# One exponential per head, a unit's matmuls moved behind the first score tile, and a feature stage in three passes

## Time and profile before

| | |
|---|---|
| median of 3 runs | 3821.25 us (3820.65 to 3821.79) |
| the profiled execution, its own time | 3822.36 us |
| its span in the profile | 3820.6 us |
| busy shares of the span | PE 95%, DVE 75%, ACT 59%, PEld 49%, POOL 12% |

### The profile page before, as it was taken

One profiled execution on the slowest core, in us unless ns is written; L12 is line 12 of the kernel. 1 busy time (PEld: TensorE's weight loads), 2 busy tenths in 40 slices (PEclk: granted clock), 3 DMA queues, 4 the chain that ended last, 5 costly groups with the idle time before them and its releaser, 6 DMA issues.

```text
span 3820.6 us, 65042 instructions
## 1 busy us (share of the span) xinstructions
PE 3613.8 (95%) x24697; PEld 1864.0 (49%) x24697; DVE 2863.1 (75%) x5691; ACT 2268.2 (59%) x2644; POOL 451.4 (12%) x486
## 2 busy tenths in 40 slices
PE   5999999999999977999999997799999999999999
PEld 3445444444444433555555555244545444454545
DVE  6878878778777776777777776487777878778775
ACT  4666666666666514666666652566666666666664
POOL 2000000000000002332323221000000000000000
PEclk9999999999999988999999997799999999999999
DMA  1000000000000000000000000000000000000000
GB/s 48 8 9 10 10 9 10 9 10 10 7 10 7 15 5 4 15 16 13 16 16 11 13 15 2 22 5 11 8 9 10 10 9 11 9 8 11 7 10 15
DMA packets 43631, 43.05 MB, mean 11 GB/s; under 512 B 16210, under 2 KB 30298, under 8 KB 43066
## 3 DMA queue, kind: packets, MB, share of 16 engines
q1 hardware_dynamic: 43322, 38.88, 3.4%
HBM read 36.38 MB, written 1.69 MB: 10 GB/s over the span
## 4 chain that ended last, share of the span: by engine, by line
PE 86%; DVE 6%; ACT 3%; issue 2%; SPq 1%; DMA 1%; POOL 1%; DVEq 0%; POOLq 0%
PE ps L592 82%; ACT work L1084 1%; DVE x L1557 1%; PE ps L929 1%; DVE over L1379 1%; PE ps L940 1%; SPq L499 1%; DMA auxQ<-mrow 1%; DVE wexp L1379 1%; PE ps L969 0%; DVE V L1287 0%; ACT Kh L1044 0%; DVE stats L1275 0%; ACT wexp L1099 0%; ACT over L1099 0%
## 5 line engine op out<-in xcount | busy, mean ns | idle before, releaser
L1356 DVE TENSOR_TENSOR acc<-acc,work 128x1024 f32<-128x1024 f32 (+2 forms) x1152 | 1386.4, 1203 | 62.0 <-ACT work L1084 18.0
L1084 ACT ACTIVATE work<-ps 128x1024 f32<-128x1024 f32 (+1 forms) x1344 | 1276.1, 996 | 201.2 <-PE ps L592 191.6
L592 PE MATMUL ps<-work,V 128*64 128x512 f32 (+3 forms) x5376 | 1233.1, 579 | 0.0
L1379 DVE CUSTOM_DVE_ANT_0 over<-ps,over,mpart 128x512 f32<-128x512 f32 (+3 forms) x642 | 423.3, 697 | 506.8 <-PE ps L592 499.9
L592 PEld LDWEIGHTS ps<-work,V 128*64 128x64 f32 x5376 | 448.9, 137 | 539.7 <-issue 444.5
L592 PE MATMUL ps<-Qh,Kh 64*128 64x512 f32 (+3 forms) x2688 | 659.0, 485 | 36.9 <-ACT work L1084 10.2
L1069 ACT ACTIVATE over<-ps 128x1024 f32<-128x1024 f32 (+1 forms) x321 | 315.9, 984 | 571.5 <-PE ps L592 571.5
L592 PE MATMUL ps<-Qh,Kl 64*128 64x512 f32 (+3 forms) x2688 | 526.8, 386 | 0.0
L592 PE MATMUL ps<-Ql,Kh 64*128 64x512 f32 (+3 forms) x2688 | 523.8, 384 | 0.0
L592 PE MATMUL ps<-auxQ,auxK 64*128 64x512 bf16 (+3 forms) x2688 | 519.7, 380 | 0.0
L1379 DVE CUSTOM_DVE_ANT_0 wexp<-ps,wexp 128x512 f32<-128x512 f32 (+1 forms) x632 | 377.0, 635 | 41.9 <-POOL wexp L1207 16.2
(11 more groups left out here) (190 smaller groups left out, 2749.6 us busy)
## 6 DMA issues: line engine op xcount, KB each, us to landing
rden<-inverse_sums SPq DMA_DIRECT2D x186, 128.0 KB, 2.9
auxQ<-mrow SPq DMA_DIRECT2D x384, 1.0 KB
wqk<-in_wqk SPq DMA_DIRECT2D x24, 128.0 KB, 2.5
dcomp<-rden SPq DMA_DIRECT2D x186, 2.0 KB
wv<-in_wv SPq DMA_DIRECT2D x24, 64.0 KB, 2.2
inverse_sums<-rcomp SPq DMA_DIRECT2D x93, 4.0 KB, 1.3
work<-in_mlp_w SPq DMA_DIRECT2D x1, 1024.0 KB
work<-in_c_aux SPq DMA_DIRECT2D x1, 1024.0 KB, 4.8
```

Source lines behind the costliest of these rows:

```text
L592: return pe.matmul(o, w, m, start=start, stop=stop, skip_group_check=True)
L1084: act.activation(work[:, 2 * e:2 * e + 2, q0:CH], ps[:, b:b + 2, q0:CH], ACT.Exp, scale=L.scale).then_inc(s["p_ready"], 1)
L1356: dve.tensor_tensor(o, o, work[:, slots[two]:slots[two] + 2, q0:CH], ALU.add).then_inc(s["acc_ready"], 1)
L1379: dve.tensor_tensor_reduce(clipped[:, h2, col:col + w], ps[:, b0 + h2, col:col + w], clipped[:, h2, col:col + w], 1.0, start, ALU.add, ALU ...
```

## The change

It has four parts.

1. On TensorE the excess of slot 0 goes behind tile 0, and on ScalarE its Relu goes behind the exponentials of tile 0 (ahead of those of tile 1).
2. A tile's exponentials are two instructions of 512 columns, one for each head. The eight matmuls of a tile are issued as head 0, head 0, head 1, head 0, head 1, head 0, head 1, head 1, and each head has its own increment of `st_ready`. The counts of `st_ready` and `p_ready` are doubled. In tiles 2 and 3 head 0 waits for its own exponential alone, head 1 for its own.
3. The feature stage does all Gelus, then all Sigmoids, then all copies, with buffers of their own for each chunk and six PSUM banks in turn for the first matmuls. Its `softmax(faw)` moves to the experts of the first layer.
4. SP's DMAs of the feature stage move into the opening of the last attention, behind the loads of the first weights.

```diff
 scores():
-    for m, (kk, qq) in enumerate(((Kh, Qh), (Kh, Ql), (Kl, Qh))):
-        for h2 in range(2):
-            mm(ps[:, 2 * two + h2, q0:CH], kk[p][head(h2), keys], qq[p][head(h2), queries], m == 0, False)
-    for h2 in range(2):
-        ins = mm(ps[:, 2 * two + h2, q0:CH], auxK[head(h2), keys], auxQ[p][head(h2), queries], False, True)
-    ins.then_inc(s["st_ready"], 1)
+    if free is not None:
+        pe.wait_ge(s["p_ready"], 2 * free - 1)
+    part(0, 0)
+    part(1, 0)
+    if free is not None:
+        pe.wait_ge(s["p_ready"], 2 * free)
+    part(0, 1)
+    part(2, 0)
+    part(1, 1)
+    part(3, 0).then_inc(s["st_ready"], 1)
+    part(2, 1)
+    part(3, 1).then_inc(s["st_ready"], 1)
 row_block():
-    if 0 in units:
-        m, u = units[0]
-        at_least(pe, s["top_ready"], L.NTOP * m + L.tops_to[u])
-        excess(m, m % 2, u, MAXB)
...
     scores(n, p, 2 * g, 0)
-    at_least(pe, s["p_ready"], tiles)
+    if 0 in units:
+        m, u = units[0]
+        at_least(pe, s["top_ready"], L.NTOP * m + L.tops_to[u])
+        excess(m, m % 2, u, MAXB)
+    at_least(pe, s["p_ready"], 2 * (tiles))
...
     if 0 in units:
         m, u = units[0]
         pe.wait_ge(s["relu_ready"], L.NR * m + L.relus_to[u] + 1)
         base(m, m % 2, u)
-    pe.wait_ge(s["p_ready"], tiles + 1)
-    scores(n, p, 2 * g + 1, 0)
-    pe.wait_ge(s["p_ready"], tiles + 2)
-    scores(n, p, 2 * g + 1, 1)
+    scores(n, p, 2 * g + 1, 0, tiles + 1)
+    scores(n, p, 2 * g + 1, 1, tiles + 2)
 ScalarE, cycle():
-    clip(0)
     if L.main(x):
         for j in range(4):
+            if j == 1:
+                clip(0)
...
-            act.activation(work[:, 2 * e:2 * e + 2, q0:CH], ps[:, b:b + 2, q0:CH], ACT.Exp,
-                           scale=L.scale).then_inc(s["p_ready"], 1)
+            act.activation(work[:, 2 * e, q0:CH], ps[:, b, q0:CH], ACT.Exp, scale=L.scale)\
+                .then_inc(s["p_ready"], 1)
+            act.wait_ge(s["st_ready"], 2 * tile + 2)
+            act.activation(work[:, 2 * e + 1, q0:CH], ps[:, b + 1, q0:CH], ACT.Exp, scale=L.scale)\
+                .then_inc(s["p_ready"], 1)
 TensorE, features():
-    pe.wait_ge(fw_ready, 1)
-    pe.transpose(ps[0:NF, 7, 0:HEADS], faw[:, 0:NF], ident[0:HEADS, 0:HEADS]).then_inc(fwT_psum, 1)
     pe.wait_ge(yt_ready, 7 * NC)
     for c in range(NC):
         for m in range(3):
...
+            at_least(pe, ft_ready, 3 * c + m - 5)
+            pe.matmul(ps[0:M, (3 * c + m) % 6, :], wext[:, m * P:m * P + M], yv[:, c * CH:(c + 1) * CH],
                       start=True, stop=True).then_inc(ft_psum, 1)
+    pe.wait_ge(fw_ready, 1)
+    pe.transpose(ps[0:NF, 7, 0:HEADS], faw[:, 0:NF], ident[0:HEADS, 0:HEADS]).then_inc(fwT_psum, 1)
+    pe.wait_ge(fw_ready, 2)
+    for c in range(NC):
+        pe.wait_ge(ft_ready, 3 * c + 3)
...
+    for c in range(NC):
+        pe.wait_ge(fs_ready, c + 1)
+        pe.matmul(ps[0:HEADS, 4 + c, :], fawT[:], fs[c], start=True, stop=True).then_inc(br_psum, 1)
 ScalarE, ahead of the last attention:
     for c in range(NC):
         for m in range(3):
...
+            act.activation(fh[c][m][0:M, :], ps[0:M, (3 * c + m) % 6, :], ACT.Gelu, bias=bext[0:M, m:m + 1])\
+                .then_inc(ft_ready, 1)
+    for c in range(NC):
+        act.wait_ge(fo_psum, c + 1)
+        act.activation(fs[c], ps[0:NF, (6 + c) % 8, :], ACT.Sigmoid, bias=b2ext[:]).then_inc(fs_ready, 1)
+    for c in range(NC):
         act.wait_ge(br_psum, c + 1)
...
+        act.activation(brow[c], ps[0:HEADS, 4 + c, :], ACT.Copy, scale=1.0 / LAYERS[2].scale).then_inc(br_ready, 1)
 SyncE, attention(), opening():
     load_pair(0, 0)
     load_out(0, 0)
     if L.featured:
+        bias_rows()
         load_bias(0, 0)
```

More of the change, by code:

```diff
@@ L344, in program @@
         small = over[:].rearrange("p m (n t e) -> p (m n) t e", t=NT, e=E_EXP)
-        brow, fs = acc[0:HEADS, 0, 0, :], acc[0:NF, 0, 1, :]
-        bparts = acc[0:HEADS, 1, 0, :].bitcast(BF16).rearrange("h (m q) -> h m q", m=2)
+        fh = [[work[:, slot if slot < 8 else slot + NC, :] for slot in range(3 * c, 3 * c + 3)] for c in range(NC)]
+        fs = [acc[0:NF, c // 2, c % 2, :] for c in range(NC)]
+        brow = [(over if c < 2 else oT)[0:HEADS, c % 2, :] for c in range(NC)]
+        bparts = [acc[0:HEADS, c // 2, c % 2, :].bitcast(BF16).rearrange("h (m q) -> h m q", m=2) for c in range(NC)]
         bT = [wm[0:2 * TPC, p, :].rearrange("r (c q) -> r c q", q=P) for p in range(2)]
@@ L557, in _ @@
             sp.wait_ge(A[1]["x_added"], NC * PAIRS)
[L558 to L566, removed]
             attention(LAYERS[2])
@@ L641, in job, with scores @@
                         ins.then_inc(s["op_ready"], 1)
-                def scores(n, p, k, two):
+                def scores(n, p, k, two, free=None):
                     c, tiles = L.steps[k]
@@ L966, in features @@
                         M = P if m < 2 else FH
-                        if c >= 1:
-                            pe.wait_ge(ft_ready, 4 * (c - 1) + m + 1)
-                        pe.matmul(ps[0:M, m, :], wext[:, m * P:m * P + M], yv[:, c * CH:(c + 1) * CH],
+                        at_least(pe, ft_ready, 3 * c + m - 5)
+                        pe.matmul(ps[0:M, (3 * c + m) % 6, :], wext[:, m * P:m * P + M], yv[:, c * CH:(c + 1) * CH],
                                   start=True, stop=True).then_inc(ft_psum, 1)
-                    pe.wait_ge(ft_ready, 4 * c + 3)
+                pe.wait_ge(fw_ready, 1)
[3 more added lines that the diff above has]
+                    pe.wait_ge(ft_ready, 3 * c + 3)
                     for m in range(3):
                         M = P if m < 2 else FH
[L974 to L980, removed]
+                        mm = pe.matmul(ps[0:NF, (6 + c) % 8, :], w2b[0:M, m, :], fh[c][m][0:M, :], start=(m == 0), stop=(m == 2))
+                    mm.then_inc(fo_psum, 1)
+                for c in range(NC):
+                    pe.wait_ge(fs_ready, c + 1)
+                    pe.matmul(ps[0:HEADS, 4 + c, :], fawT[:], fs[c], start=True, stop=True).then_inc(br_psum, 1)
             pe.wait_ge(ident_in, 16)
@@ L1077, in cycle @@
                             e = tile % RING
[L1078 removed]
+                            act.wait_ge(s["st_ready"], 2 * tile + 1)
                             if tile >= RING:
@@ L1116, in _ @@
             act.wait_ge(dl_ready, 1)
+            act.activation(faw[:, 0:NF], faw[:, 0:NF], ACT.Exp).then_inc(ex_ready, 1)
+            act.wait_ge(dl_ready, 2)
             act.activation(small[:, 2, :, :], small[:, 1, :, :], ACT.Exp).then_inc(ex_ready, 1)
@@ L1140, in _ @@
             whole_norm(6)
-            act.wait_ge(dl_ready, 2)
-            act.activation(faw[:, 0:NF], faw[:, 0:NF], ACT.Exp).then_inc(ex_ready, 1)
             for c in range(NC):
@@ L1145, in _ @@
                     M = P if m < 2 else FH
-                    act.wait_ge(ft_psum, 4 * c + m + 1)
-                    if c >= 1:
-                        act.wait_ge(ft_psum, 4 * c)
-                    act.activation(work[0:M, m, :], ps[0:M, m, :], ACT.Gelu, bias=bext[0:M, m:m + 1]).then_inc(ft_ready, 1)
-                act.wait_ge(ft_psum, 4 * c + 4)
-                act.activation(fs, ps[0:NF, 3, :], ACT.Sigmoid, bias=b2ext[:]).then_inc(ft_ready, 1)
+                    act.wait_ge(ft_psum, 3 * c + m + 1)
+                    act.activation(fh[c][m][0:M, :], ps[0:M, (3 * c + m) % 6, :], ACT.Gelu, bias=bext[0:M, m:m + 1])\
[3 more added lines that the diff above has]
+                act.activation(fs[c], ps[0:NF, (6 + c) % 8, :], ACT.Sigmoid, bias=b2ext[:]).then_inc(fs_ready, 1)
+            for c in range(NC):
                 act.wait_ge(br_psum, c + 1)
-                if c >= 1:
-                    act.wait_ge(br_out, 32 * c)
-                    act.wait_ge(bp_ready, 2 * c)
-                act.activation(brow, ps[0:HEADS, 4, :], ACT.Copy, scale=1.0 / LAYERS[2].scale).then_inc(br_ready, 1)
+                act.activation(brow[c], ps[0:HEADS, 4 + c, :], ACT.Copy, scale=1.0 / LAYERS[2].scale).then_inc(br_ready, 1)
             attention(LAYERS[2])
@@ L1546, in experts @@
                 dve.tensor_tensor(sm[5], sm[0], sm[3], ALU.mult).then_inc(mask_ready, 1)
+                link(dve.tensor_reduce(faw[:, 6:7], faw[:, 0:NF], AX.X, ALU.add))
+                link(dve.reciprocal(faw[:, 7:8], faw[:, 6:7]))
+                dve.tensor_scalar(faw[:, 0:NF], faw[:, 0:NF], faw[:, 7:8], None, ALU.mult).then_inc(fw_ready, 1)
                 dve.wait_ge(mask_ready, 2)
```

48 lines of the change are left out of this document (28 added, 20 removed).

## The result

The changed kernel takes **4109.5 us** (median of 4 runs, 4108.2 to 4113.9) where the one before takes 3821.0 in the same runs (4 runs, 3820.0 to 3821.8). The ratio is 1.0757, with a 95% interval of 1.0739 to 1.0776: 288.5 us slower. The forecast was 4123, in a range of 4030 to 4260.

A forecast was written before the change was run, and what follows sets the result against it. TensorE (PE) was taken as the bound, with 86% of the span. The profiled 3822.4 us +256 (full layers) +67 (causal layer) -21 (features) gave 4124, set to 4123 us for the runs' median; range 4030 to 4260.

The forecast's parts named there:

- The row part: Block from first to last excess: base of slot 0 waits for its late Relu, 5.35 us becomes 6.39, 1.04 us longer.
- The column part: Part of a block behind the row part: claimed to wait for nothing that the change moves, so no cost.
- The full layers' sum: Two full attention layers: 246 blocks with a wide Relu, each 1.04 us longer, +256 us (222 to 310).
- The causal layer: Causal attention layer: wide and narrow Relus +47 and +18, covered `tops` waits -12, GpSimd's cut +14; +67 us (20 to 100).
- The features: Feature stage: engines no longer take turns, first projection 21.4 us earlier, table loads counted as nothing; -21 us (-27 to -14).
- A: Rival, row part: base never waits for the Relu and finer waits close the holes; 3690 us, chance 0.08.
- both holes: PE's waits for ScalarE in each block, ahead of tile 2 and the excess of slot 1; 147 us over about 320 blocks.
- the price of a hole: PE time lost where a weight load waits for ScalarE: 0.23 us each, though the wait reads 0.39.
- B: Rival, score tiles: the shifted heads' matmuls don't pair, so a tile costs five slots; +154 us, 4277 us, chance 0.06.
- C: Rival, score tiles: weight loads of the same half are serial, 511 us, of which half or more shows; 4420 us, chance 0.04.

The follow-up runs named there:

- e9: The changed kernel with the excess of slot 0 ahead of tile 0 again, its Relu still behind tile 0's exponentials: 4193.8 us (one run).
- e7: The changed kernel with the Relu of slot 0 ahead of tile 0's exponentials again, its excess still behind tile 0: 4032.5 us.
- e1: The changed kernel with part 1 undone, excess and Relu of slot 0 first again: 3777.4 us, ratio 0.9882 to the kernel before.
- e6: The changed kernel with the Relu of slot 0 done twice in a row, the second one counted: 4688.7 us (one run).
- e12: The changed kernel with the base of slot 0 behind tile 2 instead of ahead of it: 4069.9 us (one run).
- e10: The kernel before with only parts 3 and 4 added and its own semaphore counts kept: 3802.1 us, ratio 0.9955.
- e5: e1 with the two heads' matmuls of a tile issued in turn (0,1,0,1) instead of shifted: 3779.2 us.
- e2: The kernel before with parts 3 and 4, doubled semaphore counts and a separate wait for each head: 3833.4 us, ratio 1.0032.
- e8: e2 with a single wait for both heads instead of two: 3837.0 us, ratio 1.0034 to the kernel before.
- e11: The changed kernel with one exponential for both heads, heads' matmuls in turn and semaphore counts by one, part 1 kept: 4078.4 us.
- e3: The changed kernel with one exponential for both heads, heads' matmuls in turn and semaphore counts by two, part 1 kept: 4109.1 us.

## Why the prediction held, and where it was off

**The row part.** The mechanism is the one forecast. Point by point against the timeline above: exponentials at 1.24 and 1.73 (measured 1.23, 1.72), Relu 2.22 to 3.24 (2.20 to 3.23), base at 3.29 (3.28), PE standing for about 1.0 (0.93 in this block, 268.1 / 302 = 0.89 in the mean). `tops` of slot 0 was put at 3.9 and 5.3, and the last excess at 5.89; the medians are 3.97, 5.39 and 5.90. The row part was put at 6.39; its median is 6.40. The 320 waits for the Relu, 309 for the exponentials ahead of the last excess and 11.2 us a block are as forecast. The mean of before is 5.47 and not the 5.35 of the one block that I took for all, so the growth is 0.93 and not 1.04. That e9, e7 and e1 each move with the place of the Relu, and that e6 doubles the hole, shows the cause.

**The column part, a term that was missing.** "The column part behind it waits for nothing that the change moves" is the step that failed. Block against block, the column parts of the two full layers grew by 35 us: by 38 in the 62 blocks in which the maxima of a chunk are turned into rows and sent to `auxQ`, while the others gave 3 back. The last of these DMAs lands 4.90 us behind that transposition (`ident,mcol`), in the median of either kernel. Before, the excess stood ahead of tile 0 and filled the end of that time:

```profile
430.38 0.32 PE L592 MATMUL ps<-ident,mcol 128*64 128x128 f32 x1
...
435.04 0.50 PE L592 MATMUL ps<-Kd,Qh 64*128 64x512 f32 x2
...
435.38 0.45 PE L592 MATMUL ps<-Qh,Kh 64*128 64x512 f32 x2
```

After, tile 0 is the first thing that PE has, and it waits:

```profile
464.57 0.32 PE L599 MATMUL ps<-ident,mcol 128*64 128x128 f32 x1
...
465.91 2.56 SPq L514 DMA_DIRECT2D auxQ<-mrow  x4
...
469.51 0.19 PEld L599 LDWEIGHTS ps<-Qh,Kh 64*128 64x128 f32 x2 [1.10 <-DMA auxQ<-mrow]
```

From `ident,mcol` to tile 0 it is 5.00 us in the one and 4.95 in the other; what stood between them is gone. e9 tests this: it has the Relu late but the excess first, and its column parts in the full layers are those of the kernel before to 0.2 us in the sum; its weight loads wait 13.1 us for this DMA. In e7 and e12, with tile 0 first, it is 65.7 and 68.0.

**The full layers' sum.** From the first matmul of their row parts to the end of the last, the two layers grew by 130 and 131 us, 261 against the +256 forecast. That it lies so near is luck, for two errors cancel: the row parts grew by 226 and not 256, the column parts by 35 and not 0.

**The causal layer.** Counted so, it grew by 48 against +67, inside 20 to 100. Its row parts grew by 59, where 79 was forecast. Its column parts shrank by 11, for which the forecast had 12: PE's waits for `tops` of the unit before (`mpart`) fell from 19.4 to 10.1 us in this layer. GpSimd's cut and the narrow Relus were not told apart by a run.

**The features.** -17.5 (e10) against -21. The chain of the stage in the changed kernel, in order of time (columns as in the earlier trace rows):

```profile
2570.60 13.98 PE ps L983 x24
...
2584.94 11.11 PE ps L992 x24
2596.05 0.97 PE ps L996 x2
```

The matmuls with `wext` take 14.0 and not 15.2, those with `w2b` 11.1 and not 9.6. The last ones (L996) are eight instructions in a row, 3.93 us from 2595.99, of which I had counted two. The first projection starts at 2599.84, 29.2 us behind 2570.60, and not 26.7. Then PE waits 1.55 us for the bias rows ahead of its first `Kh*Qh`, where I had half a microsecond.

ACT's table loads in this stage fell from nine to two, as counted, and each is 1.28 us long. The Trainium skill, ScalarE: Activation LUTs (What ACT_TABLE_LOAD costs), has about 2.66 us for a switch, 1.28 of it for the load and the rest for a drain; seven switches fewer would by that be 19 us, an estimate from that page, and the measured sum is near it. For the load itself page and trace agree, which the prediction had read as a difference in price. The drain isn't to be seen: Gelus that had their input ready started 0.02 us behind their load. And before, each Sigmoid waited 1.62 us for PE behind its load, so that load was covered. That the sums are alike is chance.

**The rest, -8 us.** More than half of it is only where one starts to count. The first score tile of an attention now stands ahead of an excess, and so comes 2 to 2.5 us earlier in it; the first row part starts at 63.9 us before and 63.8 after. Counted between row parts, the stage ahead of the last attention went from 185.3 to 165.5, 19.8 less, as in e10. The first two attentions are 142.2 us apart before and 138.8 after. Over the kernels of this text that gap is 138.2 to 144.0, and it is 142.6 in e10, which has all the VectorE operations that the change puts there. So those are not the cause of the 3.4 us; what is stays open.

**The rivals.** A (the base doesn't wait) fell at the Relu's end, 3.23 behind tile 0's start and not 2.6. But its price was wrong as well: e12 takes the wait away and stands at 4070, not at 3690, for ACT's late entry and `tops` are behind it. What A had right is that both holes can be closed; e1 does it with the unit first, for 25 us and not 147. So the price of a hole, 0.23 us, was wrong too: from e10 to e1 the row part falls by 0.13 us and not by 0.46. Most of what PE's loads waited was no lost time: 244.7 - 27.9 = 217 us of their waits went, and 25 us of time. On the matmuls themselves the same wait was only 11.1 us in the whole kernel before. B and C fell: the shifted heads cost nothing (e5 against e1, 3779.2 and 3777.4), pairs stay 0.23 apart, and the loads of the same half lie beside its matmuls. By the rule of the Trainium skill, TensorE: Matmul & The Clock Gate, Part 3 (The mechanism), named at C, these loads would be serial, and neither kernel shows it. The exception that this section of the Trainium skill makes, a load into the background weight buffer, would fit what the traces show.

## What to carry to other kernels

An instruction moved back on one engine's list must be followed to whoever waits for it on the next: here one slot of matmuls and its clip of 1 us, moved behind a tile and its exponentials, cost 332 us, though they filled the hole for which they were moved. Where two engines work in a ring, look at when the second one enters a block. ScalarE had 4.8 us to do in a row part of 5.3, so its first instruction had to start at once, although its busy share of 63% seemed to leave room. And ask of whatever stands first in a block what it covers: the excess was the cover of a transfer for which PE had waited 9.9 us in all.

## What the runs showed of the hardware

- TensorE's clock stayed at 1.00 with a hole of 0.9 us in a block of 11.2, and fell to 0.91 with holes of 1.85 (593.4 / 321) in blocks of 13.1; in the block shown it is 0.50 behind the hole, and the pairs are 0.42 apart. Of the 579 us that the doubled Relu cost, 325 are holes. That most of the other 254 is the clock is an estimate; no run holds the clock and keeps the holes.
- Exponentials that add two to a semaphore carried no wait of their own and had one more waiting instruction ahead of each, 1344 in all. With `st_ready` raised by two as well, this cost 31 to 35 us (e10 3802.1, e2 3833.4, e8 3837.0; e11 4078.4, e3 4109.1), or 26 to 30 by the ratios to the kernel before.
- The way from the maxima's transposition through DVE and four small DMAs to the last landing in `auxQ` took 4.90 us in the median of both kernels, with PE idle or not.
